# Expert 0's rows by one-hot products inside the routing, in a perceiver layer on one core

## What is computed

```python
logits = xf @ wg                                  # 1024 tokens, 8 experts
scores = softmax(logits)
top1 = argmax(scores)
rank = place of the token among those of its expert, in order of tokens
valid = rank < capacity                           # capacity 161
slot = where(valid, top1 * capacity + rank, trash)
buf = zeros((E * capacity + 1, D)).at[slot].set(xf)
eb = buf[:E * capacity].reshape(E, capacity, D)
h = gelu(einsum('ecd,edf->ecf', eb, W1) + b1)      # F = 2048
y = einsum('ecf,efd->ecd', h, W2) + b2
out = where(valid, y[slot], 0) * combine_w
x = x + out
```

## Time and profile before

| | us |
|---|---|
| median of 3 runs | 3262.93 (3259.77 to 3263.29) |
| the profiled execution | 3259.59 |
| its span | 3257.8 |
| TensorE busy | 3059.9 (94%) |
| VectorE busy | 1683.3 (52%) |
| ScalarE busy | 1445.1 (44%) |
| POOL busy | 115.1 (4%) |

### The profile page before, as it was taken

One profiled execution on the slowest core, in us unless ns is written; L12 is line 12 of the kernel. 1 busy time (PEld: TensorE's weight loads), 2 busy tenths in 40 slices (PEclk: granted clock), 3 DMA queues, 4 the chain that ended last, 5 costly groups with the idle time before them and its releaser, 6 DMA issues. The chain is left out here.

```text
span 3257.8 us, 61769 instructions
## 1 busy us (share of the span) xinstructions
PE 3059.9 (94%) x25814; PEld 2672.7 (82%) x25814; DVE 1683.3 (52%) x2786; ACT 1445.1 (44%) x2978; POOL 115.1 (4%) x87
## 2 busy tenths in 40 slices
PE   6899999999999999999999999999989789969997
PEld 5788888888888888888888888888746689959997
DVE  5355655565565556556565655656533765530001
ACT  3355555555555555555555555555532420011111
POOL 0000000000000000000000000000040320100000
PEclk9799999999999999999999999999999855579998
DMA  7311221121122112112211211211270000217661
GB/s 310 110 51 39 75 65 44 44 75 52 39 75 65 45 47 77 46 39 77 63 45 56 78 39 48 78 41 41 51 172 1 17 33 0 96 56 282 251 227 60
DMA packets 234822, 253.18 MB, mean 78 GB/s; under 512 B 22328, under 2 KB 169944, under 8 KB 234096
## 3 DMA queue, kind: packets, MB, share of 16 engines
q1 hardware_dynamic: 233040, 241.79, 23.2%
q0 software_dynamic: 1280, 4.20, 0.4%
q10 hardware_dynamic: 288, 4.19, 0.3%
HBM read 215.42 MB, written 34.70 MB: 77 GB/s over the span
## 5 line engine op out<-in xcount | busy, mean ns | idle before, releaser
L272 PE MATMUL fills<-wv_group,ctxT_hi 128*128 128x256 f32 x4096 | 777.1, 285 | 1.3 <-DVE ctxT_lo L477 0.6
L280 PE MATMUL fills<-ctxT_hi,wk_pairs 128*128 128x512 f32 x2048 | 703.9, 405 | 0.6 <-DVE keys L492 0.6
L272 PEld LDWEIGHTS fills<-wv_group,ctxT_hi 128*128 128x128 f32 x4096 | 644.6, 189 | 24.2 <-issue 20.3
L492 DVE SCALAR_TENSOR_TENSOR keys<-fills,bk,keys 64x512 fp32r<-64x512 f32 x512 | 383.8, 750 | 407.5 <-ACT keys L409 403.8
L272 PE MATMUL fills<-wv_group,ctxT_lo 128*128 128x256 f32 x2048 | 571.9, 279 | 0.0
L409 ACT ACTIVATE keys<-fills,bk 64x512 fp32r<-64x512 f32 x512 | 349.5, 683 | 404.4 <-PE fills L280 401.1
L280 PEld LDWEIGHTS fills<-ctxT_hi,wk_pairs 128*128 128x128 f32 x2048 | 385.6, 188 | 102.9 <-issue 23.9
L280 PE MATMUL fills<-ctxT_lo,wk_pairs 128*128 128x512 f32 x1024 | 401.3, 392 | 0.0
L485 DVE TENSOR_TENSOR values<-fills,values 128x512 fp32r<-128x512 f32 x256 | 176.6, 690 | 416.7 <-ACT values L404 416.7
L272 PEld LDWEIGHTS fills<-wv_group,ctxT_lo 128*128 128x128 f32 x2048 | 387.0, 189 | 0.0
L529 DVE TENSOR_TENSOR probsT<-probsT_ps,probsT 128x512 fp32r<-128x512 f32 x504 | 348.2, 691 | 67.4 <-ACT probsT L441 58.8
(11 more groups left out here) (210 smaller groups left out, 2999.4 us busy)
## 6 DMA issues: line engine op xcount, KB each, us to landing
e_w<-in_L_ffn_W SPq DMA_DIRECT2D x64, 1024.0 KB, 8.8
ctx_stage<-in_ctx SPq DMA_DIRECT2D x128, 256.0 KB, 2.9
wv_group<-wv_split SPq DMA_DIRECT2D x64, 512.0 KB, 4.7
wk_pairs<-wk_split SPq DMA_DIRECT2D x128, 256.0 KB, 3.3
q<-q_split SPq DMA_DIRECT2D x256, 64.0 KB, 2.7
q_split<-p_qb SPq DMA_DIRECT2D x16, 512.0 KB, 3.8
o_parts<-o_half SPq DMA_DIRECT2D x128, 64.0 KB, 1.9
a_ua<-o_parts SPq DMA_DIRECT2D x32, 256.0 KB, 5.4
```

The costliest lines, as they stand in the source:

```text
L272: last = nc.tensor.matmul(pJ[:, bank[0], 256 * k:256 * k + 256], c[:, t, s:s + P], wv[:, w, t, :], start=t + n == 0, stop=t == DT - 1 and ...
L280: last = nc.tensor.matmul(pJ[:, bank[0], :], wk[:, p, w, t, :], c[:, t, 512 * j:512 * j + 512], start=t + n == 0, stop=t == DT - 1 and n == 2)
L492: last = nc.vector.scalar_tensor_tensor(out=keys[lo_rows(j), x, 512 * j:512 * j + 512], in0=pJ[DK * a:DK * a + DK, bk_, :], scalar=bk_sb[h ...
```

## The change

Expert 0's rows no longer come from `buf`. POOL writes one more row of indices, 0 to 160, on each partition (`place`). Behind the cast of the slots VectorE compares that row with each token's slot, two groups of 128 tokens at a time: `here` is 1 where token and place agree for slots 0 to 160, which are expert 0's, and 0 elsewhere. TensorE multiplies `xn` by `here`, summed over the eight groups of tokens, one product chain for each quarter of the 512 numbers, into `pO`, a PSUM tile that the attention used earlier in the block. The result is expert 0's rows, already turned, and VectorE copies it in two halves into `route.xe`, which is now kept across the two blocks and used by all experts in place of `f_xe`. The scatter of all rows stays; POOL no longer waits for its landing at the end of its list, SP does at the beginning of its list in the experts' block (`route.sent`), and there it loads the rows of expert 1 first. The transposes, the load and the copy for expert 0 are gone.

```diff
+            place = sb("g_place", [P, CAP], F32, s6)
+            here = sb("g_here", [P, B, CAP], F32, s6)
...
+                nc.gpsimd.iota(place[:, :], pattern=[[1, CAP]], base=0, channel_multiplier=0,
+                               allow_small_or_imprecise_dtypes=True).then_inc(consts, 1)
                 pool.wait_ge(placed, 1)
                 for t in range(B):
                     nc.gpsimd.indirect_dma_start(buf[:, :], bass.IndirectOffsetOnAxis(ap=route.slot[:, t:t + 1], axis=0),
-                                                 xn[:, t, :], None).then_inc(sent, 16)
-                pool.wait_ge(sent, 16 * B)
+                                                 xn[:, t, :], None).then_inc(route.sent, 16)
...
                 nc.vector.tensor_copy(route.slot[:, :], sl[:, 0, :]).then_inc(placed, 1)
+                dve.wait_ge(consts, 5)
+                for n in range(4):
+                    two = slice(2 * n, 2 * n + 2)
+                    nc.vector.tensor_tensor(here[:, two, :], place[:, :].unsqueeze(1).to_broadcast([P, 2, CAP]),
+                                            sl[:, 0, two].unsqueeze(2).to_broadcast([P, 2, CAP]), ALU.is_equal).then_inc(marked, 1)
                 dve.wait_ge(exped, 1)
...
                 step(nc.vector.tensor_tensor(route.weight[:, :], prob[:, :], valid[:, :], ALU.mult))
+                for n in range(2):
+                    dve.wait_ge(picked, n + 1)
+                    nc.vector.tensor_copy(route.xe[:, 2 * n:2 * n + 2, :],
+                                          pO[:, n, :].rearrange("p (c s) -> p c s", c=2)[:, :, 0:CAP]).then_inc(taken, 1)
...
                 nc.tensor.matmul(pc.rearrange("p b e -> p (b e)"), ones[:, :], flat,
                                  start=True, stop=True).then_inc(counted, 1)
+                for c in range(DT):
+                    for t in range(B):
+                        if c == 0 and t % 2 == 0:
+                            pe.wait_ge(marked, t // 2 + 1)
+                        last = nc.tensor.matmul(pO[:, c // 2, 256 * (c % 2):256 * (c % 2) + CAP], xn[:, t, P * c:P * c + P],
+                                                here[:, t, :], start=t == 0, stop=t == B - 1)
+                    if c % 2:
+                        last.then_inc(picked, 1)
...
-            xe = sb("f_xe", [P, DT, CAP], F32, s2)
+            xe = route.xe
...
-                rows_load(0)
+                sp.wait_ge(route.sent, 16 * B)
+                rows_load(1)
                 for c in range(FC):
                     w1_load(sp, 1, c)
...
                 for e in range(E):
-                    if e + 1 < E:
-                        sp.wait_ge(xt, e + 1)
+                    if e and e + 1 < E:
+                        sp.wait_ge(xt, e)
                         rows_load(e + 1)
...
-                    if f == 0:
-                        pe.wait_ge(x_ready, e + 1)
+                    if f == 0 and e:
+                        pe.wait_ge(x_ready, e)
...
-                rows_turn(0)
                 for e in range(E):
                     for f in range(NF):
                         up_tile(e, f)
...
-                rows(0)
```

More of the change, by code:

```diff
@@ L1363, in self_attention @@
             shifted, exped, hot, counted = (sem(n) for n in ("g_shifted", "g_exped", "g_hot", "g_counted"))
-            placed, sent, consts, b_turned, b_out = (sem(n) for n in ("g_placed", "g_sent", "g_consts", "g_bt", "g_bout"))
+            placed, consts, b_turned, b_out = (sem(n) for n in ("g_placed", "g_consts", "g_bt", "g_bout"))
+            marked, picked, taken = sem("g_marked"), sem("g_picked"), sem("g_taken")
             block = s6.enter_context(nc.Block())
@@ L1594, with __init__ @@
 class Route:
-    def __init__(self, slot, yslot, weight, b1T, b2T):
+    def __init__(self, slot, yslot, weight, b1T, b2T, xe, sent):
         self.slot, self.yslot, self.weight, self.b1T, self.b2T = slot, yslot, weight, b1T, b2T
+        self.xe, self.sent = xe, sent
 class ExpertWeights:
@@ L1686, in rows_turn @@
                 def rows_turn(e):
-                    pe.wait_ge(eb_in, 32 * e + 32)
+                    pe.wait_ge(eb_in, 32 * e)
                     if e >= 2:
@@ L1762, in rows @@
                 def rows(e):
-                    dve.wait_ge(xt, e + 1)
+                    dve.wait_ge(xt, e)
                     nc.vector.tensor_copy(xe[:, :, :], pt[:, :, :].rearrange("p b (c s) -> p (b c) s", c=2)[:, :, 0:CAP]
@@ L1838, in perceiver @@
             route = Route(left("e_slot", [P, B], U32), left("e_yslot", [P, B], U32), left("e_weight", [P, B], F32),
-                          left("e_b1T", [P, E * F // P], F32), left("e_b2T", [P, E * DT], F32))
+                          left("e_b1T", [P, E * F // P], F32), left("e_b2T", [P, E * DT], F32),
+                          left("e_xe", [P, DT, CAP], F32), nc.alloc_semaphore("e_sent"))
             weights = ExpertWeights(nc, W1, W2, right)
```

## The result

The changed kernel takes **3252.0 us** (median of 10 runs, 3248.18 to 3255.15); the kernel before, run beside it, 3261.48 (10 runs, 3258.88 to 3263.29). The ratio is 0.9969 with a 95% interval of 0.9960 to 0.9978: some 10 us less, by the interval 7 to 13. The forecast was 3253.2 in a range of 3250.0 to 3258.5, a gain of 9.7. Sign, size and range came out; two steps of the working did not: how long the picks take, and what POOL still holds at the end of the block. In each of the two traces of the change one of them hides the other.

What follows compares the result with a forecast made beforehand. TensorE, 94% busy, was taken to set the pace. Expert 0's products starting 8.3 us earlier plus 1.4 from the clock gave 9.7, so 3262.93 - 9.7 = 3253.2 us, range 3250.0 to 3258.5.

Steps and rivals of the forecast that it cites:

- What bounds the kernel: TensorE, 94% busy, sets the pace; the kernel's end moves with expert 0's product start, plus those products' own gain or loss.
- The marks: VectorE's four comparisons of slots with places, 0.49 us each; TensorE starts at about 2912.7 and doesn't wait again.
- The rival that POOL's issues would hold VectorE: Comparisons run only behind POOL's eighth scatter issue; expert 0 starts at 2934.2 or 2940.9, 0.6 or 8.7 us slower; chance 0.04.
- The picks: TensorE's 32 products forming expert 0's rows: 10.3 us, the first 3 at 1.2 GHz; bounds 8.8 and 17.0.
- the rival of low clock throughout: The products forming expert 0's rows stay at 1.2 GHz, 17.0 us; gain 1.6 or 3.0, middle 2.3, 3260.6 us; chance 0.08.
- The copy and the hand-over: Copy out of PSUM with product tail 0.6 us, then 0.3 between the blocks; expert 0's products start at 2923.9.
- The rival of a longer hand-over for TensorE: TensorE enters the experts' block up to 3.3 us late; with the clock falling too, gain 5.0, 3257.9 us; chance 0.10.
- POOL is done at 2922.47, so it isn't last: At the routing block's end POOL's eighth scatter issue ends at 2922.47, ahead of the experts' start at 2923.9.
- what is removed: For expert 0 alone: scatter wait, row load, eight transposes and copy, all between POOL's first issue and 2932.24.
- The clock at expert 0: Expert 0's up products run wholly at 2.4 GHz: 17.6 us instead of 19.04, gaining 1.4.
- the clock falls at the hand-over: TensorE's 0.9 us rest before the experts lowers its clock for 3.5 us; 1.7 lost, gain 8.0, 3254.9; chance 0.19.
- Queues and weights: SP's loads for expert 1 go out as before from 2925.4; eleven microseconds are left, so this costs nothing.

Runs made afterwards that it cites:

- the second trace: The unaltered change run and traced once more, against the kernel before: 3251.34 us, ratio 0.9972.
- picks twice: The change with all 32 pick products made twice, the first pass into a PSUM tile nobody reads: 3260.33 us, ratio 1.0002 to the kernel before.
- scatter moved: The change with POOL's eight scatter issues moved from the routing's block into the experts' block: 3251.61 us, ratio 0.9971 to the kernel before.
- the two with the scatter moved: The change with POOL's scatter issues in the experts' block, without and with unread products warming TensorE ahead of the picks: 3251.61 and 3250.95 us.
- POOL waits: The change with POOL again waiting for the scatter's landing at the end of its list: 3253.7 us, ratio 0.9975 to the kernel before.
- faster picks: The change with ten unread products keeping TensorE busy ahead of the picks: 3254.18 us, ratio 0.9980 to the kernel before.
- the run with the layout alone: The kernel before with only the change's memory layout, new tiles allocated and never written: 3259.53 us, ratio 0.9996.

## Why the prediction was right, and where it wasn't

**What bounds the kernel: right.** The start of expert 0's products moved, and all behind it moved with it. 8.65 to 9.09 us added to that start came out as 9.0 at the end (picks twice).

**The marks: right.** Four comparisons took 1.72 us, 0.43 each (0.49 forecast). TensorE started 0.62 us behind the start of the cast (forecast 0.7). The rival that POOL's issues would hold VectorE falls: the four take 1.72 us with POOL's issues beside them and 1.70 where POOL issues nothing (scatter moved). The Trainium skill's SBUF — State Buffer, Who interferes with whom, lets a VectorE instruction with two inputs in SBUF collide with a POOL instruction that reads SBUF, and not with one that only writes it; these two figures agree, if writing descriptors reads nothing there, which no run here shows.

**The picks: a term that was mis-sized in one trace.** 10.3 us were forecast, with 3 us at 1.2 GHz. At 0.138 a record at 2.4 GHz and 0.265 at 1.2, the 10.25 us of the second trace are 11 records, or 3.0 us, at the low level, and the 11.53 of the first are 21, or 5.6 us. The other runs whose picks start at low clock fall on the same two: 10.34 and 10.20, 11.40 and 11.39. When the clock rises varies from execution to execution by 2.6 us, and it costs up to 1.3. The bounds held; the rival of low clock throughout did not occur.

**The copy and the hand-over: right.** 0.49 us for the copy, and 0.29 to 0.30 from its end to TensorE's first record wherever nothing else is late (the first trace of the change, picks twice, and the two with the scatter moved). The rival of a longer hand-over for TensorE falls: in all nine traces in which TensorE's first product in the block waits for nothing, it starts 0.02 to 0.03 us behind SP's first issue. The Trainium skill's Runtime: NRT & Kernel Launch, Instruction fetch mechanics, makes a taken branch stall for a fetch if its target lies outside what was fetched ahead. No such stall is seen at this opening; whether the target lay outside, no run shows.

**"POOL is done at 2922.47, so it isn't last": wrong.** This is the step that failed, and with it an item of "what is removed": the wait for the scatter is not gone. The end of POOL's last record was taken for the end of POOL's part in the block. The block's end drains POOL until the scatter has landed: DRAIN ends 2.1 us behind the last record, and the block opens 0.2 us later. (Before the change, too, the landing, 2921.51 + 2.7 = 2924.2, came 1.1 us ahead of the load that the prediction took for its sign.) In three kernels whose copy is done in time, the up products start 2.34, 2.33 and 2.35 us behind the end of POOL's last record, at a distance of 12.8. With POOL moved out it is 0.30 behind the copy. The start is thus the later of two: the copy's end + 0.30, or 12.8. With picks of 10.25 POOL is last (12.79 instead of the 11.9 forecast), and with picks of 11.53 the copy is (13.23), by 0.4. The two hide each other: in the first trace the long picks explain the start by themselves, in the second POOL does, and neither start alone tells of both. The hand-over gave 7.0 and 7.5 us in the two traces, and not 8.3.

**The clock at expert 0: right, with less room than was said.** 1.47 us against 1.4. It held over rests of 1.07 and 1.92 us. It fell after 2.37 (POOL waits) and 3.38 (faster picks). Each of these is one execution, and as the clock's rise varies, its fall may too. The rival "the clock falls at the hand-over" was one edit away: in the trace with POOL's wait put back it came true.

**Queues and weights: right.** SP's first row load comes at 13.20, before 13.38, and expert 1 follows without a gap.

**The sum.** Hand-over and clock measure 8.5 us in the first trace and 8.9 in the second, where 9.7 were forecast. The medians differ by 9.5, and the ratio makes it 10.1. The traces' remainder, 2.1 and 0.7 us, lies ahead of the cast and behind the up products, where the change edits nothing on the path. It can be the spread of executions (from the end of expert 0's up products to the end of the span the changed kernels' traces differ among themselves by 1.6 us, 305.7 to 307.3), or the new places of the buffers; the run with the layout alone doesn't exclude a microsecond or two. So about a microsecond of the agreement isn't explained, and stays open: that the medians came out within 0.2 us of the 9.7 is in part luck.

## What to carry to other kernels

When a step is taken off the path, price everything else that must end at the same border, to the microsecond, and look for it in the sequencers' records at the block's own line, too. Here taking a wait out of POOL's list did not take the waiting away: the block's end waited for the landing of POOL's indirect DMAs all the same. What took it off the path was to move the issues into the next block, where nobody needed them early. Before a step is made faster, look at what ends beside it: here 1.4 us off the picks turned into a rest, and in that trace the rest into 1.7 us of lower clock. Work that flows into the next work without a long gap was worth its clock here, and some filling in the gap held it where the gap couldn't be closed.

## What the runs showed of the hardware that wasn't expected

POOL's DRAIN at the end of a block ended 0.4 us behind the landing of the indirect DMAs that POOL had issued there, without a wait in the program; the landing came 1.7 us behind the last DMA's record in five traces and 5.7 to 5.9 behind it in the two with the scatter moved. With a wait for the landing ahead of it, DRAIN ended 0.9 us behind the landing. A dense stream of the same products, begun at 1.2 GHz behind the same idle time (4.2 us, on TensorE), was granted 2.4 GHz after 3.0 us in some executions and after 5.6 in others.
